# Two packed attentions: queries' and keys' parts by direct SBUF transfers, and three sets of slots

## The chip, the cores and the metric

One core of a Trainium2 chip runs the whole program in one launch. The time is the device time of an execution in microseconds (us); of several runs the median is given. PE is the engine of the matmuls, DVE, ACT and POOL work elementwise, SP only issues DMAs; ACT can issue DMAs too, on a queue of its own (ACTq; SP's is SPq).

## The reference

Eight layers run one after the other on x of 4 x 256 tokens by 128. The change concerns two of them, both attentions, which the kernel computes with one function:

```
L0: masked attention, 8 heads of 16; queries from x, keys and values from the context
    k, v = split((ctx @ W_src.T + b_src) * mask);  q = (tgt @ W_tgt.T + b_tgt) * mask
    out = softmax(q k^T / sqrt(16), masked keys at -inf) v;  [tgt, out] @ W_out.T + b_out
L1: unmasked attention, 16 heads of 8; keys and values are 256 rows of context, then 256 of x
    q, k, v from x @ w_qkv.T;  out = softmax(q k^T / sqrt(8)) v;  out @ w_proj.T + b_proj
```

Between them lies a layer of routed experts (four rounds), behind them five layers more, which the change leaves as they are. Sums are in f32.

## The kernel before

Both attentions come from packed_attention(). A query or key in f32 is split into three bf16 parts, high, middle and low (qp and kp, [128 partitions, 1024 tokens] each; a partition is one dimension of one head). The product of two such numbers is made of six terms (TERMS: pairs of part numbers), and all six are done by one matmul with a longer contraction: for a head, the six terms lie below each other on partitions. These stacks are the slots: QS and KS hold for one b (256 tokens) all heads, row r * HD + d on the partitions for term r and dimension d, heads and tokens along a row. Masked: HD = 16, 96 rows and one for the mask. Unmasked: HD = 8, 48 rows, twice (SIDES = 2: heads lie on partitions 0 and up, and on 64 and up), and KS also takes the parts of the context. Three more rows take the row maxima of the scores, in bf16 parts as well, so that the second product comes out with the maximum subtracted.

Getting the parts into the slots moves them across partitions. The kernel before goes by way of DRAM. Each term row of each half of the tokens is stored from 128 partitions (line 318): the keys by SP into k_dram, the queries by ACT into q_dram. SP waits for the stores and loads slots: masked, load_terms (line 674), seven DMAs for each b; unmasked, load_rows (line 664), in two shares of two sides for keys, queries and context each, twelve DMAs for a b. The masked attention has a set of slots for each of the four b (BUFS = 4), the unmasked one has BUFS = 2 and reloads them.

Then a software pipeline runs on all engines over the steps i (masked 16 steps, unmasked 64): first_pass (PE, line 368) makes scores of step i, DVE takes their row maxima (line 802), and once a unit of half a b is done, PE turns its maxima (425), which are split into parts (masked: ACT 539 and 571, DVE 816 and 823; unmasked: ACT 543 and POOL 623 to 628), and SP brings them to their slot rows by 2 KB transfers from SBUF to SBUF (line 733: three for a unit, six in the unmasked case). second_pass (PE, line 382) makes the scores again, LAG steps behind, after its wait for these transfers; ACT takes the exponential (555), PE multiplies by the values (412). Each engine's program is one fixed order; PE's order puts second_pass of step i - LAG behind first_pass of step i, and ahead of the next ones.

SP's order is written out by hand: for the unmasked attention the context of b = 0, the stores of the keys' first half, the loads of b = 0 (first share), the stores of the second half, all other loads of the first BUFS b, and then the loop over units v with the transfers of maxima (line 733), a piece of later weights (l1v, line 3428), and, from v = 2 on, the loads of b + 1 ahead of the unit's maxima. The buffers NMp of the maxima's parts are two, so the parts of unit v are written only after the transfers of unit v - 2.

ACT's part of the start is in scalar(): for each of the two halves it casts the first and the second part (lines 505 and 509), then issues the stores of the queries (three masked, six unmasked), and only then goes on with the next half. DVE subtracts (764 and 769). The slots are first filled with ones by POOL (those of the unmasked attention in the rounds, at line 1550, once a step).

Of the kernel before, what the change touches and what calls it, by code (L numbers as in the profile page):

```python
# [151 lines left out]
def packed_attention(k, name, number, NH, HD, key_tiles, masked, eps, W, ahead=None, split=None):  # L152
# [22 lines left out]
    BUFS = B if masked else 2  # L175
    SHARES = 1 if masked else 2
# [4 lines left out]
    SPS = SLOTS // SHARES  # L181
    HPS = NH // SHARES
# [21 lines left out]
    vtmp = k.carve(F32, HALF)  # L204
    mark = k.carve_mark()
    q32, k32 = k.carve(F32, T), k.carve(F32, T)
    qp = [k.carve(BF16, T) for _ in range(3)]
    kp = [k.carve(BF16, T) for _ in range(3)]
# [12 lines left out]
    q_dram, k_dram = k.q_dram[number], k.k_dram[number]  # L221
# [4 lines left out]

    fill_done = count("fill_done", BUFS + 1 if masked else 1)
    q_psum = count("q_psum", 2)
# [7 lines left out]
    STORES = 16 * (3 if masked else 6)  # L236
    stored_k = count("stored_k", 2 * STORES)
    stored_q = [count(f"stored_q{h}", STORES) for h in range(2)]
    c_stored = k.c_stored

    if masked:
        loaded = [[count(f"loaded{i % 2}{i // 2}", k.loads_of(name))] for i in range(BUFS)]
    else:
        loaded = [[count(f"loaded{i}{j}", 2 * k.loads_of(name)) for j in range(SHARES)] for i in range(BUFS)]
# [79 lines left out]
    def tensor(pe):  # L324
# [112 lines left out]
        for i in range(ALL + LAG + 1):  # L437
            s = i - LAG
            if i < ALL:
                b, u = divmod(i, STEPS)  # L440
                if u % (STEPS // SHARES) == 0:
                    pe.wait_ge(*loaded[b % BUFS][u // (STEPS // SHARES)].at(k.loads_of(name) * (b // BUFS + 1)))
                first_pass(b, PER * u)
# [50 lines left out]
    def scalar(act):  # L494
        k.norm.scalar(act, use, k.xnT)

        for pair in range(2):
# [12 lines left out]
            parts, cols = piece(2 * pair + 1)[2:]  # L510
# [36 lines left out]
        for i in range(ALL + LAG + 1):  # L547
# [11 lines left out]
            if s > 0 and s % key_tiles == 0:  # L559
                hg = s // key_tiles  # L560
                if hg == 1:
                    act.wait_ge(*stored_k.at(2 * STORES))
                    act.wait_ge(*stored_q[0].at(STORES))
                    act.wait_ge(*stored_q[1].at(STORES))
# [81 lines left out]
    def sync(sp):  # L646

        def store_half(h):
            for i in range(3):
                if i < 2:  # L650
                    sp.wait_ge(*part.at((first_of, last_of)[i](2 * h)))
                else:
                    sp.wait_ge(*rest.at(last_of(2 * h)))
                parts, cols = piece(2 * h)[2:]
                for row in [i] if masked else K_ROWS[i]:
                    store(sp, k_dram, NH, parts[i], row, cols).then_inc(stored_k.semaphore, 16)

        def load_rows(dram, dst, first, b, share, done):

            slots = slice(share * SPS, (share + 1) * SPS)  # L660
            for side in range(SIDES):
                h = share * HPS + side * SPS
                src = dram.rearrange("(h r) t -> r h t", h=NH)[:, h:h + SPS, b * S:(b + 1) * S]
                sp.dma_start(dst[rows_at(side, R_MASK), slots, first:first + S], src).then_inc(done, 16)

        def load_terms(dram, dst, b, parts, done):

            src = dram.rearrange("(h r) t -> r h t", h=NH)[:, :, b * S:(b + 1) * S]
            at = 0
            while at < len(parts):  # L670
                n = 1
                while at + n < len(parts) and parts[at + n] == parts[at] + n:
                    n += 1
                sp.dma_start(dst[at * HD:(at + n) * HD, :, :], src[parts[at] * HD:(parts[at] + n) * HD]).then_inc(done, 16)
                at += n

        def load_context(b, share):
            sp.wait_ge(c_stored, 16 * 6)
            load_rows(k.c_dram, KS[b % BUFS], 0, b, share, loaded[b % BUFS][share].semaphore)

        def load(b, share):
            done = loaded[b % BUFS][share].semaphore
            if b == 0:
                sp.wait_ge(*stored_k.at(STORES))
                sp.wait_ge(*stored_q[0].at(STORES))
            if b == 2:
                sp.wait_ge(*stored_k.at(2 * STORES))
                sp.wait_ge(*stored_q[1].at(STORES))
            if b >= BUFS:
                sp.wait_ge(*p2_psum.at(STEPS * (b - 2) + STEPS // SHARES * (share + 1)))  # L690
            if masked:
                load_terms(k_dram, KS[b], b, [term[1] for term in TERMS], done)
                load_terms(q_dram, QS[b], b, [term[0] for term in TERMS], done)
            else:
                load_rows(k_dram, KS[b % BUFS], NK - S, b, share, done)
                load_rows(q_dram, QS[b % BUFS], 0, b, share, done)
            if not masked and b > 0:
                load_context(b, share)

        if masked:  # L700
            sp.wait_ge(k.mask_ready, 1)
            for b in range(BUFS):
# [3 lines left out]
                    .then_inc(loaded[b][0].semaphore, 16)  # L706
        else:
            sp.wait_ge(*k.slots_filled.at(4))
            for share in range(SHARES):
                load_context(0, share)  # L710
        store_half(0)
        load(0, 0)
        store_half(1)
        for share in range(1, SHARES):
            load(0, share)
        for b in range(1, BUFS):
            for share in range(SHARES):
# [564 lines left out]
def routed_rounds(k, name, number, E, W, ahead):  # L1282
# [49 lines left out]
    k.slots_filled = k.count("packed_fill_done", 4)  # L1332
# [208 lines left out]
    def gpsimd(pool):  # L1541
        k.norm.gpsimd(pool, use)
        for g in range(ITEMS):
# [4 lines left out]
            if FILL_AT <= g < FILL_AT + 4:  # L1548
# [1618 lines left out]
class Kit:  # L3167


    def __init__(self, nc, ctx, dram):  # L3170
# [30 lines left out]
        self.q_dram = {n: dram["scratch"](f"q_parts{n}") for n in (0, 2)}  # L3201
        self.k_dram = {n: dram["scratch"](f"k_parts{n}") for n in (0, 2)}
# [112 lines left out]

    def loads_of(self, name):

        return 16 * (3 + 4 + 1 if name == "l0x" else 6)
# [140 lines left out]

def pick(width):  # L3460
# [25 lines left out]
def pack(i):  # L3486
# [4 lines left out]
    w["l0x"] = [tiles(src[:D].T), tiles(src[D:].T), f["L0_xattn_W_tgt"].T, wo[:, :D].T, tiles(slots(wo[:, D:].T, 8)),  # L3491
                pick(16), f["L0_xattn_b_src"][:D, None], f["L0_xattn_b_tgt"][:, None],
                across(f["L0_xattn_b_src"][D:]), across(f["L0_xattn_b_out"])]
    qkv = f["L1_xattn_w_qkv"]
    w["l1x"] = [qkv[D:2 * D].T, qkv[2 * D:].T, qkv[:D].T, tiles(slots(by_steps(f["L1_xattn_w_proj"].T), 16)), pick(8),
# [51 lines left out]
```

## Time and profile before

| | us |
|---|---|
| median of 3 runs (range) | 1118.69 (1116.24 to 1119.89) |
| the profiled execution, its own time | 1116.3 |
| its span, first to last instruction | 1114.5 |
| masked attention, about | 10 to 91 |
| rounds of routed experts, about | 91 to 295 |
| unmasked attention, about | 295 to 454 |
| PE busy | 979.7 (88%) |
| DVE busy | 823.2 (74%) |
| ACT busy | 636.2 (57%) |
| POOL busy | 426.2 (38%) |

The profile is of one execution. Its lines give the busy time of groups of instructions; a timeline gives for a stretch each engine's instructions in order, with the idle time in front and what ended it. The issue of a DMA by SP or ACT is a piece of time on SPq or ACTq; it isn't counted as busy time of an engine. The chain is followed back from the last instruction to what released each step.

### The profile page before, as it was taken

The page shows a single profiled execution, that of the slowest core. Times are in us where ns is not written, and L with a number is a line of the kernel's source. Part 1 is how long each engine was busy: PE and PEld are TensorE (multiplying, and loading weights), DVE is VectorE, ACT ScalarE, POOL GpSimd, SP SyncE. Part 2 cuts the span into 40 slices and gives each one's busy share as a digit, 9 for nine tenths or more (in the row PEclk, how much of TensorE's full clock was granted, in tenths as well). Part 3 has the DMA queues.
Part 4 walks back from the last instruction along what each step waited for, and adds up shares of the span by engine and source line. Part 5 has one row for each costly group of instructions (what it writes and reads, how often), then busy time and mean ns, then how long its engine had stood idle before and what let it go on. Part 6 is the DMA issues. An engine that isn't in the chain of part 4 may idle for free.

```text
span 1114.5 us, 18229 instructions
## 1 busy us (share of the span) xinstructions
PE 979.7 (88%) x5958; PEld 720.5 (65%) x5958; DVE 823.2 (74%) x1980; ACT 636.2 (57%) x1594; POOL 426.2 (38%) x664
## 2 busy tenths in 40 slices
PE   5688999999759998868999999996899999998587
PEld 4457887888513434746777777775667777777465
DVE  7855898898667881698989988768665667675663
ACT  3373666766317775366797877973144666664121
POOL 8231122111121110235766767767130565654200
PEclk9697999999859998899999999997899999999789
DMA  5530211122052310300000000303000100003000
GB/s 215 139 122 1 76 39 39 39 67 62 20 170 81 98 40 20 152 1 1 1 1 1 1 1 1 151 1 121 1 1 21 57 1 2 1 14 138 1 1 20
DMA packets 32254, 53.55 MB, mean 48 GB/s; under 512 B 4192, under 2 KB 24448, under 8 KB 31008
## 3 DMA queue, kind: packets, MB, share of 16 engines
q1 hardware_dynamic: 29616, 50.03, 13.5%
q10 hardware_dynamic: 2544, 2.36, 0.7%
q8 instruction: 48, 0.79, 0.3%
q14 instruction: 46, 0.38, 0.1%
HBM read 45.33 MB, written 6.88 MB: 47 GB/s over the span
## 4 chain that ended last, share of the span: by engine, by line
PE 64%; DVE 16%; ACT 9%; issue 6%; DMA 2%; POOL 1%; SPq 1%; DVEq 0%; ACTq 0%
PE psum L1733 8%; PE psum L1356 8%; PE psum L1366 7%; ACT region_d L1795 4%; PE psum L2524 3%; PE psum L1763 3%; PE psum L2453 3%; PE psum L412 3%; PE psum L368 2%; DVE region_d L1931 2%; ACT region_c L1812 2%; PE psum L1719 2%; PE psum L2427 2%; PE psum L2469 2%; DVE null_work L2626 2%
## 5 line engine op out<-in xcount | busy, mean ns | idle before, releaser
L1733 PE MATMUL psum<-gated_parts 128*128 128x512 f32 x768 | 191.1, 400 | 18.7 <-DVE region_d L1931 15.1
L1733 PEld LDWEIGHTS psum<-gated_parts 128*128 128x128 f32 x768 | 137.0, 188 | 69.1 <-DVE region_d L1931 36.8
L2024 POOL TENSOR_TENSOR region_d<-region_d 128x256 f32<-128x256 f32 x126 | 94.6, 751 | 93.1 <-DVE region_d L1931 91.0
L1425 ACT ACTIVATE rounds_work<-psum,region_c 128x512 f32<-128x512 f32 x128 | 84.6, 688 | 28.1 <-PE psum L1356 25.9
L802 DVE TENSOR_REDUCE work<-psum 128x1 f32<-128x512 f32 x128 | 81.8, 686 | 22.0 <-PE psum L368 20.3
L1356 PE MATMUL psum<-parts,split 128*128 128x512 f32 x384 | 95.9, 400 | 0.0
L1366 PE MATMUL psum<-parts,split 128*128 128x512 f32 x384 | 93.3, 392 | 0.0
L1547 POOL CAST parts<-rounds_work 128x1024 fp32r<-128x1024 f32 x32 | 33.4, 1043 | 151.9 <-ACT rounds_work L1425 151.9
L1795 ACT ACTIVATE region_d<-psum,gated_work 128x128 f32<-128x128 f32 x256 | 75.9, 447 | 26.8 <-issue 22.2
L1479 DVE TENSOR_TENSOR parts<-rounds_work,parts 128x1024 fp32r<-128x1024 f32 x64 | 76.3, 1220 | 16.9 <-POOL parts L1547 15.9
L1795 ACT ACTIVATE region_d<-psum,ctx 128x128 f32<-128x128 f32 x256 | 73.0, 375 | 25.2 <-PE psum L1733 15.4
L2549 ACT ACTIVATE null_work<-psum,null_work 128x257 f32<-128x257 f32 x128 | 59.6, 471 | 43.8 <-DVE null_work L2613 43.8
L1356 PEld LDWEIGHTS psum<-parts,split 128*128 128x128 f32 x384 | 73.1, 192 | 15.5
L1366 PEld LDWEIGHTS psum<-parts,split 128*128 128x128 f32 x384 | 71.5, 188 | 14.7
L1931 DVE SCALAR_TENSOR_TENSOR region_d<-psum,gated_work,region_d 128x128 f32<-128x128 f32 x256 | 71.8, 344 | 11.6 <-ACT region_d L1795 7.5
L1931 DVE SCALAR_TENSOR_TENSOR region_d<-psum,ctx,region_d 128x128 f32<-128x128 f32 x256 | 71.9, 343 | 8.8 <-ACT region_d L1795 6.2
L555 ACT ACTIVATE work<-psum 128x1024 f32<-128x1024 f32 x64 | 65.2, 1024 | 22.1 <-PE psum L382 20.1
L2613 DVE TENSOR_REDUCE null_work<-psum 128x2 f32<-128x514 f32 x64 | 44.1, 689 | 32.3 <-PE psum L2453 32.3
L2738 POOL TENSOR_TENSOR null_work<-null_work 128x512 f32<-128x512 f32 x64 | 66.5, 1039 | 0.0
L368 PE MATMUL psum<-work 48*128 48x512 bf16 x128 | 51.7, 438 | 13.8 <-DMA work<-q_parts 10.7
L133 POOL TENSOR_TENSOR rstd<-var_eps,minus_half 128x4 f32<-128x4 f32 x12 | 12.3, 1024 | 126.3 <-DVE var_eps L93 126.2
L368 PEld LDWEIGHTS psum<-work 48*128 48x128 bf16 x128 | 12.2, 96 | 52.1 <-DVE work L802 33.0
(450 smaller groups left out, 2190.6 us busy)
## 6 DMA issues: line engine op xcount, KB each, us to landing
rounds_work<-cw_rows SPq DMA_DIRECT2D x32, 256.0 KB, 3.4
region_a<-in_l1v SPq DMA_DIRECT2D x8, 512.0 KB, 4.0
region_b_last<-in_l1o SPq DMA_DIRECT2D x1, 4096.0 KB, 12.3
region_a<-in_l2f SPq DMA_DIRECT2D x1, 4096.0 KB, 12.0
region_b_last<-in_l3f_small SPq DMA_DIRECT2D x1, 4096.0 KB, 12.8
region_a<-in_l3f SPq DMA_DIRECT2D x1, 2080.0 KB, 7.4
region_c<-in_l0f SPq DMA_DIRECT2D x1, 2076.0 KB, 12.3
region_c<-in_l3x SPq DMA_DIRECT2D x1, 2048.0 KB, 7.8
```

What stands on the lines that cost most here:

```text
L368: ins = pe.matmul(bank[g % 2][:, j * NK:(j + 1) * NK], QS[b % BUFS][rows_at(side, R_MAX), slot, t * P:(t + 1) * P], KS[b % BUFS][rows_at(s ...
L555: act.activation(PT[s % 2].rearrange("p (a n) -> p a n", a=2), k.pair(2 + 2 * (s % 2)), ACT.Exp, scale=scale).then_inc(p2_exp.semaphore, 1)
L802: dve.tensor_reduce(NM[:, b, heads[0]:heads[0] + HPG, t], bank[g % 2][:, :].rearrange("p (j n) -> p j n", j=HPG), AX.X, ALU.max, negate=Tr ...
L1356: ins = pe.matmul(bank[f], w1_part[a][:, e, f * P:(f + 1) * P], cur_part[b][:, half_of(s % 2)], start=n == 0, stop=n == len(PASSES) - 1)
L1366: ins = pe.matmul(bank[4 + g % 2], w2_part[a][:, g % E, f, :], hidden_part[b][g % 2][:, f, :], start=f == 0 and n == 0, stop=f == FT - 1 a ...
L1425: act.activation(H[g % 2][:, f, :], bank[f], ACT.Gelu_apprx_tanh, bias=W("b1")[:, (g % E) * FT + f:(g % E) * FT + f + 1]).then_inc(h_ready ...
L1479: dve.tensor_tensor(two(hidden_part[1][g % 2], c), two(H[g % 2], c), two(hidden_part[0][g % 2], c).bitcast(F32), ALU.subtract).then_inc(h_ ...
L1733: ins = pe.matmul(bank[2 * (n % 2) + c], src[a][:, t * P:(t + 1) * P], weights[b][:, piece(c)], start=m == 0, stop=m == len(PASSES) - 1)
L1795: ins = act.activation(scaled[n % RING][:, e, :], bank[2 * (n % 2)][:, e * P:(e + 1) * P], ACT.Copy, scale=scalars[:, n % NT, e:e + 1])
L1931: ins = dve.scalar_tensor_tensor(out=tile, in0=bank[2 * (n % 2) + 1][:, e * P:(e + 1) * P], scalar=scalars[:, n % NT, HALF_E + e:HALF_E + ...
L2024: pool.tensor_tensor(tile[:, 0:2, :], tile[:, 0:2, :], tile[:, 2:4, :], ALU.add).then_inc(k.pool_chain, 1)
L2738: pool.tensor_tensor(PR[g % 4][:, :, 0:S], PR[g % 4][:, :, 0:S], r.broadcast_to([P, TPB, S]), ALU.mult)\
```

## The change

It sends the parts straight from qp and kp to the slots, from SBUF to SBUF. For each part, each term row that uses it, each side and each b there is one transfer (to_slots), 128 or 64 partitions of 256 tokens to HD partitions by all the heads of a side. For that the projections' columns are reordered on the host (inside_out, by_sides) so that heads run fastest inside a dimension. ACT issues the queries of b = 0, SP everything else; the stores, k_dram and q_dram go, and so do the waits for them. The unmasked attention gets three sets of slots (BUFS = 3), all loaded ahead of the loop over the units; the loads of b = 3 stand in that loop, keys and context at v = 3 and queries at v = 4. One wait for the whole of a b takes the place of one for each share. ACT casts the second half without issuing anything for it. The third set of slots is filled by two more memsets of POOL in the rounds. The buffers qp and kp no longer lie under those that the pipeline uses.

```diff
-    BUFS = B if masked else 2
-    SHARES = 1 if masked else 2
+    BUFS = B if masked else 3
+    DIRECT = 2 * len(TERMS) * SIDES
+    LOADS = 16 * (DIRECT + (1 if masked else 4))
...
+    def to_slots(queue, what, b, i):
+
+        parts, slots, first = (kp, KS, NK - S) if what == "k" else (qp, QS, 0)
+        for r in (K_ROWS if what == "k" else Q_ROWS)[i]:
+            for side in range(SIDES):
+                at = side * SIDE + r * HD
+                queue.dma_start(slots[b % BUFS][at:at + HD, :, first:first + S],
+                                parts[i][side * (P // SIDES):(side + 1) * (P // SIDES), b * S:(b + 1) * S])\
+                    .then_inc(loaded[b % BUFS].semaphore, 16)
...
-                for row in [i] if masked else Q_ROWS[i]:
-                    store(act, q_dram, NH, parts[i], row, cols).then_inc(stored_q[pair].semaphore, 16)
+                if pair == 0:
+                    if i == 0:
+                        act.wait_ge(*slots_ready)
+                    to_slots(act, "q", 0, i)
...
+        def load(b, what):
             for i in range(3):
+                parts_made(what, b // 2, i)
+                to_slots(sp, what, b, i)
...
-        store_half(0)
-        load(0, 0)
-        store_half(1)
-        for share in range(1, SHARES):
-            load(0, share)
-        for b in range(1, BUFS):
-            for share in range(SHARES):
-                load(b, share)
+            load_context(0)
+        for b in range(BUFS):
+            load(b, "k")
+            if b > 0:
+                load(b, "q")
+                if not masked:
+                    load_context(b)
         for v in range(UNITS * B):
             b, heads, _ = unit_of(v)
-            if BUFS <= b + 1 < B and b > 0:
-                load(b + 1, v % UNITS)
+            if BUFS < B and v == UNITS * (BUFS - 1) - 1:
+                sp.wait_ge(*p2_psum.at(STEPS * (B - BUFS)))
+                load(B - 1, "k")
+                load_context(B - 1)
+            if BUFS < B and v == UNITS * (BUFS - 1):
+                load(B - 1, "q")
...
-            if FILL_AT <= g < FILL_AT + 4:
+            if FILL_AT <= g < FILL_AT + 6:
```

## Rows read from the trace of the kernel before

**Rows 1.** The page, part 4: shares of the chain that ended last.

```profile
PE 64%; DVE 16%; ACT 9%; issue 6%; DMA 2%; POOL 1%; SPq 1%; DVEq 0%; ACTq 0%
```

**Rows 2.** The chain, unmasked start: start us, us, what.

```profile
308.03 2.69 DMA q_parts<-work
...
312.11 3.34 DMA work<-q_parts
```

**Rows 3.** Timeline of PE; columns: start us, us, engine line op tiles xcount [idle before <-releaser].

```profile
34.06 1.01 PE L368 MATMUL psum<-front_work 97*128 97x256 bf16 x4 [4.86 <-DMA front_work<-q_parts]
...
315.58 0.61 PE L368 MATMUL psum<-work 48*128 48x512 bf16 x2 [10.66 <-DMA work<-q_parts]
...
333.57 0.71 PE L382 MATMUL psum<-work 51*128 51x256 bf16 x3
```

**Rows 4.** Timeline of SP's queue (SPq), masked attention.

```profile
19.38 2.31 SPq L318 DMA_DIRECT2D k_parts<-front_work  x3
...
43.61 6.53 SPq L733 DMA_DIRECT2D front_work<-front_work  x9
```

**Rows 5.** Single lines: engine op xcount: issue ns min/median/max, first and last start.

```profile
L733 SPq DMA_DIRECT2D work<-work x48: 634/635/692, 328.3 to 420.5; - x48
...
L318 SPq DMA_DIRECT2D k_parts<-work x12: 528/614/960, 303.0 to 316.5; - x12
...
L664 SPq DMA_DIRECT2D work<-k_parts x16: 308/443/536, 310.8 to 384.6; - x16
...
L1558 SPq DMA_DIRECT2D cw_rows<-rounds_work x8: 264/265/284, 110.1 to 267.5; - x8
```

**Rows 6.** Timeline of SP's queue, unmasked attention.

```profile
302.95 3.82 SPq L318 DMA_DIRECT2D k_parts<-work  x6
...
322.16 0.93 SPq L664 DMA_DIRECT2D work<-k_parts  x2
...
328.34 4.13 SPq L733 DMA_DIRECT2D work<-work  x6
...
359.04 0.85 SPq L664 DMA_DIRECT2D work<-k_parts  x2
...
367.05 4.43 SPq L733 DMA_DIRECT2D work<-work  x6
...
379.51 4.05 SPq L733 DMA_DIRECT2D work<-work  x6
```

**Rows 7.** Timelines of ACT and of DVE, masked attention.

```profile
23.15 1.15 ACT L505 ACTIVATE front_work<-front_work 128x512 bf16<-128x512 f32 x2 [2.18 <-issue]
...
46.85 0.27 ACT L539 ACTIVATE front_work<-psum 8x128 bf16<-8x128 f32 x1 [1.80 <-DMA front_work<-front_work]
...
34.68 1.29 DVE L802 TENSOR_REDUCE front_work<-psum 128x2 f32<-128x512 f32 x2 [2.38 <-PE psum L368]
...
47.22 0.27 DVE L816 TENSOR_TENSOR front_work<-psum,front_work 8x128 f32<-8x128 f32 x1
```

**Rows 8.** Timelines of ACT and of DVE, unmasked start.

```profile
308.70 1.09 ACT L505 ACTIVATE work<-psum 128x512 bf16<-128x512 f32 x2 [3.47 <-issue]
...
310.71 1.29 DVE L769 TENSOR_TENSOR work<-work 128x512 bf16<-128x512 f32 x2
316.20 11.02 DVE L802 TENSOR_REDUCE work<-psum 128x1 f32<-128x512 f32 x16 [4.20 <-PE psum L368]
```

**Rows 9.** The chain, 356 to 375 us: the fourth unit's maxima reach PE.

```profile
370.84 1.68 DMA work<-work
```

**Rows 10.** The page, part 5: POOL's casts in the rounds, busy, mean, idle before.

```profile
L1547 POOL CAST parts<-rounds_work 128x1024 fp32r<-128x1024 f32 x32 | 33.4, 1043 | 151.9 <-ACT rounds_work L1425 151.9
```

**Rows 11.** DMA queue q1: packets, MB, share of 16 engines, 31:45 and 342.3:346.3.

```profile
q1 hardware_dynamic: 5892, 3.01, 92.5%
...
q1 hardware_dynamic: 64, 0.01, 1.2%
```

**Rows 12.** Stretch 316:334: us, busy (x) by engine, PEclk, DMA share, GB/s.

```profile
316.00:334.00 18.00, 15.21 (x34) 3.71 (x33) 15.57 (x24) 0.68 (x3) 1.92 (x6) 0.50 0.48 136
```

More of the change, by code:

```diff
@@ L203, in packed_attention @@
     NMf = [k.carve(F32, P) for _ in range(2)]
-    vtmp = k.carve(F32, HALF)
+    vtmp = k.carve(F32, HALF) if masked else None
+    if not masked:
+        qp, kp = ([k.carve(BF16, T) for _ in range(3)] for _ in range(2))
     mark = k.carve_mark()
     q32, k32 = k.carve(F32, T), k.carve(F32, T)
-    qp = [k.carve(BF16, T) for _ in range(3)]
-    kp = [k.carve(BF16, T) for _ in range(3)]
+    if masked:
+        qp, kp = ([k.carve(BF16, T) for _ in range(3)] for _ in range(2))
     k.carve_back(mark)
@@ L235, in packed_attention @@
     c_rest = count("c_rest", 2 if masked else 0)
-    STORES = 16 * (3 if masked else 6)
-    stored_k = count("stored_k", 2 * STORES)
-    stored_q = [count(f"stored_q{h}", STORES) for h in range(2)]
     c_stored = k.c_stored
[L241 to L244, printed above, removed]
+    loaded = [count(f"loaded{i % 2}{i // 2}", (B - i + BUFS - 1) // BUFS * LOADS) for i in range(BUFS)]
     v_sb = count("v_sb", B)
@@ L440, in tensor @@
                 b, u = divmod(i, STEPS)
-                if u % (STEPS // SHARES) == 0:
-                    pe.wait_ge(*loaded[b % BUFS][u // (STEPS // SHARES)].at(k.loads_of(name) * (b // BUFS + 1)))
+                if u == 0:
+                    pe.wait_ge(*loaded[b % BUFS].at(LOADS * (b // BUFS + 1)))
                 first_pass(b, PER * u)
@@ L560, in scalar @@
                 hg = s // key_tiles
[L561 to L564, printed above, removed]
+                if masked and hg == 1:
+                    for b in range(B):
+                        act.wait_ge(*loaded[b].at(LOADS))
                 act.wait_ge(*av_done.at(hg * key_tiles))
@@ L646, in sync @@
     def sync(sp):
-        def store_half(h):
-            for i in range(3):
[L650 to L677, printed above, removed]
-            sp.wait_ge(c_stored, 16 * 6)
-            load_rows(k.c_dram, KS[b % BUFS], 0, b, share, loaded[b % BUFS][share].semaphore)
@@ L681, in load, with parts_made @@
[L681 to L698, printed above, removed]
+        def parts_made(what, half, i):
+            m = 2 * half + (what == "q")
+            if i < 2:
+                sp.wait_ge(*part.at((first_of, last_of)[i](m)))
+            else:
+                sp.wait_ge(*rest.at(last_of(m)))
@@ new lines, in load, with load_context @@
+        def load(b, what):
+            for i in range(3):
+                parts_made(what, b // 2, i)
+                to_slots(sp, what, b, i)
+        def load_context(b):
+            sp.wait_ge(c_stored, 16 * 6)
+            for share in range(2):
+                slots = slice(share * SLOTS // 2, (share + 1) * SLOTS // 2)
+                for side in range(SIDES):
+                    h = share * NH // 2 + side * SLOTS // 2
+                    src = k.c_dram.rearrange("(h r) t -> r h t", h=NH)[:, h:h + SLOTS // 2, b * S:(b + 1) * S]
+                    sp.dma_start(KS[b % BUFS][rows_at(side, R_MASK), slots, 0:S], src).then_inc(loaded[b % BUFS].semaphore, 16)
@@ L1331, in routed_rounds @@
     high_pool = k.count("rounds_h_high", ITEMS)
[L1332 removed]
+    k.slots_filled = k.count("packed_fill_done", 6)
     FILL_AT = 8
```

26 lines of the change are left out of this document (11 added, 15 removed).

## The prediction

> **What bounds the kernel now.** I read the page's chain first: PE holds 64% of the path, DMA only 2% [rows 1]. So a change that touches only DMAs can win what the two packed attentions wait for at their starts, and little more. The chain of the unmasked attention shows it: the parts are stored (2.69 us to land), then loaded back (3.34 us) [rows 2], and PE starts its first scores at 315.58 after 10.66 us of idle; in the masked one it starts at 34.06 after 4.86 us, released by a DMA too [rows 3]. After that no load of slots is waited for again.
>
> The second view is SP's own timeline, since SP issues most of what the change replaces. SP works in order, and the 2 KB transfers of the maxima (L733) stand behind the slot loads in its program: masked, behind the loads of all four b; unmasked, behind those of the first BUFS of them. Their first issue is at 43.61 [rows 4] and at 328.34 [rows 6]. The question is what stands ahead of them after the change.
>
> **The price of one direct transfer.** The trace of before has no transfer from 128 (or 64) partitions to 16 (or 8) partitions of SBUF. Its nearest rows [rows 5]: SBUF to SBUF, L733, takes the queue 0.634 us though it moves only 2 KB; SBUF to DRAM from 128 partitions with the heads split off, L318, 0.614 us; DRAM to slots, L664, 0.443 us. The least on SP is L1558, 0.264 us. Between two issues lie 0.044 us (a pair of L664 takes 0.93 [rows 6]). I take L733's price, because both ends are SBUF as in the change: a pitch of 0.634 + 0.044 = 0.68 us. Bounds: 0.49 (L664's median) and 0.74 (L733's longest, 0.692). The context loads stay at 0.487.
>
> **Masked attention.** Removed: 6 stores on SP, 6 on ACT, 28 loads on SP. Added: 6 transfers on ACT (q of b = 0) and 42 on SP (k of b = 0, then k and q of three b, 6 each). SP is free for them at 19.38, behind its mask transfers [rows 4]. So the first transfer of maxima is issued at 19.38 + 42 x 0.68 = 47.94 instead of 43.61: 4.3 us later. Who waits: ACT's L539 for the third unit writes into a buffer that this transfer reads; it started at 46.85, released by a DMA; DVE's L816 at 47.22 needs it, and the next row maxima stand behind it in order [rows 7]. There was no slack (L816 shows no idle before it: DVE came to it straight from the row maxima), so DVE is late by 4.3 us, and PE and ACT with it.
>
> The gain at this stage's start is swallowed by that. It would be: DVE sits idle for 2.38 us before the maxima at 34.68 [rows 7], so it could start them at 32.30. ACT now has six transfers of q to issue, not three, ahead of its casts at 23.15, which move by some 1.3 us (an estimate: three more at 0.68, less the waits that lie between the present three); DVE, which needs them and has other work meanwhile, passes on some 0.8. The maxima start about 1.6 us earlier, and then stop at the third unit until the same time as above. Masked: +4.3 us; 42p - 24.2 in general for a pitch p, but never below -1.6.
>
> **Unmasked attention.** Removed: 12 stores on SP, 12 on ACT; 32 loads. Added: 12 transfers on ACT and 12 on SP for b = 0 (two sides each), and 24 each for b = 1, 2 and 3 on SP. With three sets, the loads of b = 0, 1 and 2 all stand ahead of the first transfer of maxima: 12 + 24 + 24 direct ones and 8 for the context (those of b = 0 are out long before). From SP's first store now, at 302.95 [rows 6]: 302.95 + 60 x 0.68 + 8 x 0.487 = 347.65, instead of 328.34: 19.3 us later. PE's first second_pass (L382) started at 333.57 [rows 3], 5.2 us after that issue, when the six had landed; it stands in PE's order ahead of further first passes, so DVE and ACT run dry too. It now starts at about 352.9. LAG is unchanged, so the first pass has got no further by then, and nothing is made up: +19.3 us, 60p - 21.5 in general.
>
> The gain at the start is hidden under it again, and small: ACT casts at 308.70, after waiting 3.47 us for its own six issues; six more at 0.68 make that 312.8, and DVE's last part moves from 312.0 to about 316.1, against maxima that start at 316.20 now [rows 8]. The store's and the load's landing go, ACT's longer issue is late next: -0.1 us, which the sum leaves out.
>
> Later: the loads of b = 3. SP is let go for them by the count that lets it go at 359.04 now. Then 12 x 0.68 + 4 x 0.487 = 10.1 us stand ahead of the transfers of unit 3, which go out at 367.05 [rows 6], with the chain running through them to the landing at 372.52 and on to PE [rows 9]. They go at 369.15: +2.1 us. The 12 for q come behind them: 369.15 + 4.6 + 8.2 = 381.9, against 379.51 + 2.1 = 381.6 for unit 4: +0.3. Together +2.4.
>
> POOL's two more memsets of slots fall in the rounds, where it sits idle 151.9 us in front of 32 casts, 4.7 us each [rows 10]; nothing, unless a cast came late by their length. The weight columns are reordered on the host. The third set brings b = 2 forward, but no load was waited for in the steady part: nothing.
>
> **DMA engines.** The slots take the same 512 B packets as before, and the stores go. Between 31 and 45 us 5892 packets kept 16 engines busy 92.5%, 35 ns each; the maxima's small packets from SBUF to SBUF took 12 ns (1.2% of 4 us for 64) [rows 11]. A masked transfer has 128 packets, 8 per engine, 0.28 us; that is below 0.68, so the issue bounds it.
>
> **Sum.** 4.3 + 19.3 + 2.4 = 26.0 us. Against the profiled execution (1116.3 us, span 1114.5) that is 1142.3; the median of the three runs lies 2.4 above it, inside their scatter of 3.7. I take 1118.7 + 26.0 = 1144.7, rounded to 1144.
>
> **Rivals.**
> 1. *A direct transfer is issued like a load from DRAM* (pitch 0.49). For: L664 splits heads and rows as the new destination does. Against: L733 and L318, whose two sides are cut differently, as the new ones are. Masked -1.6, unmasked 60 x 0.49 - 21.5 = +7.9, later 0: 1125.
> 2. *Not slower: the issue is cheap and the landings decide.* At L664's least, 0.308 (pitch 0.35), the masked start gains all of 2.4, the maxima's transfers go out at 302.95 + 60 x 0.35 + 3.9 = 327.9, 0.4 earlier: 1116. At L1558's 0.264 (pitch 0.31) they go at 325.5 and 2.9 us are kept: 1113. It decides below a pitch of 0.38, and is faster by over 0.3% below 0.34. Against: none of these rows splits a partition axis.
> 3. *The packets bound it.* If a packet of 512 B from SBUF to SBUF took 0.12 us, 8 per engine would take 0.96 us; 60 of them instead of 40.8 us take 57.6, 16.8 more, and masked 42 take 11.8 more: about 1173. It decides above 85 ns a packet. Against: 35 and 12 ns.
> 4. *The maxima don't wait*, because the order isn't as I read it: masked -1.6, unmasked -0.1, 1117. The diff leaves their loop behind the loads.
>
> The Trainium skill (DMA: Bandwidth & Descriptors, "Issuing engines are not separate DMA queues") calls the time a sequencer takes to start a DMA "usually small relative to the DMA itself". By that rule rival 2 would hold, at 1113 to 1116; rows 5 and 11 speak against it. The same page ("Why a DMA increments its semaphore by 16 and not by 1") lets a DMA use at most as many engines as divide the slowest dimension of both its sides, which would be 8 for the unmasked slots and would halve rival 3's room; no row here shows that number.
>
> **Chances.** Forecast, pitch 0.58 to 0.74 (+14 to +34: 1133 to 1152): 0.70. Rival 1: 0.13. Rival 2: 0.09. Rival 3: 0.06. Rival 4: 0.02. The range takes in the forecast and rival 1: 1124 to 1154, 0.83. Some 0.3% (3.4 us) can be told from no change. Faster: rival 2 below 0.34, 0.05. Same: the rest of it, rival 4 and a corner of rival 1, 0.07. Slower: 0.88.
>
> The granted clock was 0.50, the level of 1.2 GHz, from 316 to 334 after PE's idle [rows 12]. The new idle falls where the clock was low anyway; I add nothing, though it may cost 1 or 2 us more.
>
> **What would show it.** SP: an unbroken row of direct issues from 303 to about 348 (shifted by what the masked stage lost), each near 0.63 us, and L733 only behind it. PE: an idle of some 19 us before the first L382 of the unmasked attention, released by DMA or SP. ACT: the third L539 of the masked one at about 51. It is wrong if the issues take below 0.55 us, if PE starts that L382 at 330 to 335, or if the DMA share stands near full while SP waits.

## The result and the profile after

| | before | after |
|---|---|---|
| median, runs made together (range) | 1119.29 (1116.24 to 1121.01) | 1146.1 (1143.48 to 1153.77) |
| ratio, 95% interval | | 1.0257 (1.0225 to 1.0289) |
| profiled execution, its own time | 1116.3 | 1143.48 |
| span | 1114.5 | 1141.7 |
| mean granted clock | 0.936 | 0.921 |

The changed kernel is 26.8 us slower by the medians and 27.2 us by the two spans. In the changed kernel L321 is the direct transfer, L709 the maxima's transfer (it was L733), L387 the second pass (L382), L373 the first pass (L368), L673 the context's load.

The page's chain first. SP's DMA issues, 1% of it before [rows 1], now hold 6%; the page puts 4% on L321 alone:

```profile
PE 61%; DVE 14%; ACT 9%; issue 6%; SPq 6%; POOL 1%; ACTq 1%; DMA 1%; DVEq 0%; POOLq 0%
```

The next lines are single lines of the kernel (ns of one issue: least, median, most), which answer rows 5:

```profile
L321 SPq DMA_DIRECT2D work<-work x84: 608/609/936, 306.6 to 403.7; - x84
L321 SPq DMA_DIRECT2D front_work<-front_work x42: 547/598/1169, 19.3 to 46.4; - x42
L321 ACTq DMA_DIRECT2D work<-work x12: 624/705/1154, 308.6 to 316.9; - x12
```

SP's timeline, masked and then unmasked, which answers rows 4 and 6:

```profile
19.30 27.67 SPq L321 DMA_DIRECT2D front_work<-front_work  x42
...
306.61 24.70 SPq L321 DMA_DIRECT2D work<-work  x36
331.36 1.90 SPq L673 DMA_DIRECT2D work<-ctx_parts  x4
333.31 15.61 SPq L321 DMA_DIRECT2D work<-work  x24
348.96 2.13 SPq L673 DMA_DIRECT2D work<-ctx_parts  x4
351.13 4.08 SPq L709 DMA_DIRECT2D work<-work  x6
...
391.86 4.08 SPq L709 DMA_DIRECT2D work<-work  x6
...
406.35 4.08 SPq L709 DMA_DIRECT2D work<-work  x6
```

The queue never rests between 306.61 and 355.21. The first maxima go out 44.52 us behind the first issue of the stage, where before it was 328.34 - 302.95 = 25.39 [rows 6]. The maxima of unit 3 are then 24.8 us behind those of before (391.86 against 367.05), those of unit 4 26.8 (406.35 against 379.51); from there on the distance stays at 26.8.

PE's timeline at the second pass, which answers the third row of rows 3; the number in brackets is the idle time in front:

```profile
356.32 0.61 PE L387 MATMUL psum<-work 51*128 51x256 bf16 x4 [17.59 <-DMA work<-work]
...
397.05 0.39 PE L387 MATMUL psum<-work 51*128 51x256 bf16 x4 [2.09 <-DMA work<-work]
```

Both idles end with a landing of maxima, not of slots: the view of L709 names PE's L387 as waiting for it, 20.7 us in three waits, and the view of L321 names nobody. Stretches around them (us, busy by engine in the order PE, PEld, DVE, ACT, POOL, then the granted clock, DMA share, GB/s):

```profile
338.80:356.00 17.20, 0.00 (x0) 0.00 (x0) 0.66 (x1) 1.11 (x1) 0.00 (x0) 0.50 0.20 56
356.30:366.00 9.70, 9.32 (x68) 2.97 (x68) 6.13 (x10) 5.54 (x7) 1.00 (x4) 0.61 0.18 56
385.00:396.80 11.80, 9.87 (x101) 3.78 (x100) 8.83 (x14) 7.14 (x9) 1.41 (x4) 1.00 0.22 61
397.50:405.00 7.50, 7.50 (x55) 2.97 (x54) 4.47 (x7) 4.10 (x5) 0.00 (x0) 0.54 0.35 110
```

While SP issues without a pause, the DMA engines are 20% busy: it is the issuing that takes the time, not the moving. And behind the short idle of 2.09 us PE runs at 0.54 of its clock for some 7 us, which nothing in the prediction had foreseen at this place.

At the starts, ACT and DVE, masked (answers rows 7) and unmasked (rows 8):

```profile
50.26 0.27 ACT L545 ACTIVATE front_work<-psum 8x128 bf16<-8x128 f32 x1 [5.49 <-DMA front_work<-front_work]
50.56 0.28 DVE L792 TENSOR_TENSOR front_work<-psum,front_work 8x128 f32<-8x128 f32 x1 [3.54 <-ACT front_work L545]
...
308.56 9.05 ACTq L321 DMA_DIRECT2D work<-work  x12
317.65 1.09 ACT L510 ACTIVATE work<-psum 128x512 bf16<-128x512 f32 x2 [8.81 <-issue]
...
320.88 4.07 DVE L778 TENSOR_REDUCE work<-psum 128x1 f32<-128x512 f32 x6
```

### The profile page after: what moved, and what is told of

It reads as the page before. It is cut to its first block, busy times and chain, and to the rows that moved or that the text cites. A ratio compares the mean times of both kernels' runs of the same rounds, so it can differ in the third digit from the quotient of the medians.

```text
span 1141.7 us, 18274 instructions
## 1 busy us (share of the span) xinstructions
PE 986.7 (86%) x5958; PEld 725.4 (64%) x5958; DVE 823.5 (72%) x1980; ACT 637.6 (56%) x1594; POOL 430.1 (38%) x666
## 4 chain that ended last, share of the span: by engine, by line
PE 61%; DVE 14%; ACT 9%; issue 6%; SPq 6%; POOL 1%; ACTq 1%; DMA 1%; DVEq 0%; POOLq 0%
PE psum L1709 9%; PE psum L1332 7%; PE psum L1342 7%; SPq L321 4%; ACT region_d L1771 4%; PE psum L2500 3%; PE psum L2429 3%; PE psum L1739 3%; PE psum L417 2%; DVE region_d L1907 2%; ACT region_c L1788 2%; PE psum L1695 2%; PE psum L2403 2%; PE psum L2445 2%; DVE null_work L2602 2%
## 5 line engine op out<-in xcount | busy, mean ns | idle before, releaser
L1709 PE MATMUL psum<-gated_parts 128*128 128x512 f32 x768 | 193.9, 405 | 16.6 <-DVE region_d L1907 12.8
L1709 PEld LDWEIGHTS psum<-gated_parts 128*128 128x128 f32 x768 | 139.3, 191 | 67.6 <-DVE region_d L1907 34.4
L373 PE MATMUL psum<-work 48*128 48x512 bf16 x128 | 52.6, 451 | 14.8 <-ACT work L514 11.1
L387 PE MATMUL psum<-work 51*128 51x256 bf16 x256 | 36.2, 288 | 20.7 <-DMA work<-work 20.7
```

What stands on the lines that cost most here:

```text
L1709: ins = pe.matmul(bank[2 * (n % 2) + c], src[a][:, t * P:(t + 1) * P], weights[b][:, piece(c)], start=m == 0, stop=m == len(PASSES) - 1)
```

## The experiments

The theory: SP issues one after the other at 0.65 to 0.69 us, and what stands ahead of the maxima's transfers in its program decides when the second pass starts. Rivals: the transfers themselves (their number, their form, the engines' load) slow the stage wherever they stand; or the third set of slots does. Several runs each, of kernels made together with runs of the kernel before.

### One attention at a time

`e1_masked_alone`: the masked attention as changed, the unmasked one by the old function.

```diff
- stages.append(packed_attention(k, "l1x", ...))
+ stages.append(packed_by_dram(k, "l1x", ...))
```

> The masked attention sends its parts directly, the unmasked one goes by DRAM with two sets as before. Theory A (SP's queue: 42 direct issues at a pitch of 0.66 us stand ahead of the first transfer of maxima): that transfer goes out at about 47.0 us instead of 43.6, the third unit's cast starts at about 50.3 instead of 46.9, and the kernel is 3.4 us slower (1122 to 1123). Theory B (the lost microseconds of the masked attention are made up later, and the whole loss is the unmasked one's): no change, within 1 us.

Measured: 1119.36 us against 1116.45, ratio 1.0025 (1.0005 to 1.0044), so 2.8 us. SP's timeline of this kernel:

```profile
19.10 28.01 SPq L321 DMA_DIRECT2D front_work<-front_work  x42
```

The interval is 0.6 to 4.9 us: it holds the 3.4 of theory A and doesn't quite shut out theory B's "within 1 us". The maxima's transfers begin at 47.15, and the unmasked attention's first store at 306.67, 3.7 us behind that of before [rows 6]. One pair of traces doesn't settle such a distance, though. In the five traces whose masked attention is that of before (before, e2, e3, e9, e10), the first maxima go out between 43.61 and 45.44, and the unmasked attention's first issue on SP stands anywhere from 302.38 to 308.17; in the four with 42 direct issues (the changed kernel twice, e1, e5) the maxima go out between 47.01 and 47.60. The means of the two groups are 2.8 us apart, which is what e1's runs give.

`e2_unmasked_alone`: the other way round.

```diff
- stages.append(packed_attention(k, "l0x", ...))
+ stages.append(packed_by_dram(k, "l0x", ...))
```

> The unmasked attention sends its parts directly with three sets, the masked one goes by DRAM as before. Theory A: first transfer of maxima of the unmasked attention 44.5 us after SP's first direct issue, second pass 19 us later than before, then 2 us at unit 3 for SP's queue and 2 us more behind it while the clock is down: 23 us slower (1141 to 1143). Theory B: 27 us slower, all of the loss.

Measured: 1145.32 us, ratio 1.0236 (1.0184 to 1.0288), so 26.3 us with 6 to either side. The first maxima's transfer stands 352.30 - 308.17 = 44.1 us behind the first issue, as in the whole change:

```profile
308.17 24.68 SPq L321 DMA_DIRECT2D work<-work  x36
...
352.30 4.54 SPq L709 DMA_DIRECT2D work<-work  x6
```

The two parts make 0.25% + 2.36% = 2.6%, the whole 2.57%: they add up within these intervals, and some nine tenths lie in the unmasked one. The 23 us of theory A and the 27 us of theory B are both inside the interval. In its profiled execution the distance to before is 18.7 us at the first maxima and 26.0 at unit 3 (398.32 - 308.17 against 367.05 - 302.95): 2 of the 7.3 between them are unit 3's issues, the rest came in a stretch of low clock behind the main idle (granted 0.67 over 357 to 386) that was longer than in the changed kernel's execution. The interval takes in both. The same trace has a short wait at unit 3 as well, and it cost more than in the changed kernel: PE waits 3.13 us at 403.54, the granted clock is 0.50 from there to 420 and 0.82 over 420:430, and the maxima of unit 4 fall 15.73 us behind those of unit 3 (before 12.46), those of unit 5 another 16.60 behind them (before 12.65).

### The third set of slots by itself

`e3_three_sets_alone`: the kernel before, still by way of DRAM, with three sets of slots.

```diff
-    BUFS = B if masked else 2
+    BUFS = B if masked else 3
```

> Both attentions by DRAM as before, only the unmasked one has three sets, with the loads of b = 2 ahead of the loop over the units. Theory A (only the number of issues ahead of the maxima counts, at 0.487 us for a load from DRAM): 12 loads more, so SP is free at 325.0 + 5.8 = 330.9 instead of waiting until 328.3: 2.5 us slower. Theory B (the third set is where the loss is, whatever the price of an issue): 10 us or more slower. Theory C (three sets are worth something by themselves): faster.

Measured: 1122.84 us, ratio 1.005 (1.0015 to 1.0084), so 5.6 us (1.7 to 9.4): theory A's 2.5 lies inside, theory B's 10 or more does not. SP's timeline:

```profile
302.44 3.75 SPq L319 DMA_DIRECT2D k_parts<-work  x6
...
330.11 4.12 SPq L734 DMA_DIRECT2D work<-work  x6
```

The first maxima go out 27.7 us behind the first store, 2.3 more than before: 12 more loads at 0.487 are 5.8 us, and SP had waited for the maxima's parts from 325.04 to 328.34 before [rows 6], which takes 3.3 of them. So the third set costs some 2 us at this place with cheap loads; with direct transfers it puts 24 of them and four context loads ahead, 24 x 0.67 + 4 x 0.49 = 18 us. It is not the set by itself but what its filling puts in front, at this price.

### The same transfers in another order

`e4_order`: the changed kernel, every direct transfer kept, but on SP part of those of later b are moved behind the maxima of earlier units: masked, the 6 queries of b = 3; unmasked, everything of b = 2 and 3, in portions.

```diff
-        for b in range(BUFS):
-            load(b, "k")
-            if b > 0:
-                load(b, "q")
-                if not masked:
-                    load_context(b)
+        behind = {}
+        if masked:
+            for b in range(B):
+                load(b, "k")
+                if 0 < b < B - 1:
+                    load(b, "q")
+            behind = {2: [(B - 1, "q", 0)], 3: [(B - 1, "q", 1), (B - 1, "q", 2)]}
+        else:
+            load(0, "k")
+            load(1, "k"); load(1, "q"); load_context(1)
...
+            for v, n in ((1, 14), (2, 11), (3, 12), (4, 11), (5, 8)):
...
         for v in range(UNITS * B):
+            for one in behind.get(v, ()):
+                issue(*one)
```

> The changed kernel with all its direct transfers, in another order on SP: masked, the queries of b = 3 behind the maxima of the first two units; unmasked, only b = 0 and 1 ahead of the first maxima, and the transfers of b = 2 and 3 dealt out in portions of 8 to 14 between the units. Theory A (order and price on SP's queue are the whole loss): no stall before the first second pass; the masked start gains 1 us, the unmasked start loses 1 us to ACT's dearer issues: within 2 us of the kernel before (1117 to 1121). Theory B (direct transfers themselves are slow to land or crowd the DMA engines): at least 10 us slower than before still.

Measured: 1123.43 us, ratio 1.0058 (1.0027 to 1.0088). SP's timeline:

```profile
19.20 23.90 SPq L323 DMA_DIRECT2D front_work<-front_work  x36
43.14 4.14 SPq L737 DMA_DIRECT2D front_work<-front_work  x6
...
300.48 24.41 SPq L323 DMA_DIRECT2D work<-work  x36
324.94 1.90 SPq L692 DMA_DIRECT2D work<-ctx_parts  x4
326.91 4.08 SPq L737 DMA_DIRECT2D work<-work  x6
```

The masked maxima go out at 43.14 (before 43.61), the first unmasked ones 26.4 us behind the stage's first issue (before 25.4, changed 44.5). Of 2.57% only 0.58% are left. This is the run that decides between the theory and the first rival: as many transfers, of the same form, on the same queue, and nearly four fifths of the loss are gone. The time is above the 1117 to 1121 of theory A; the loss of 3 to 10 us that the interval allows stays below the 10 us and more of theory B.

`e4_again`: the same kernel, one execution more.

> The same kernel as e4_order once more, for its trace: its runs lay between 1116.6 and 1129.8 us, and the longer ones had a lower mean granted clock. Theory A (SP's order is put right and what is left is the clock's doing): whatever the time, the transfers of maxima go out at the same distances from SP's first direct issue as in the first trace, except where the granted clock is at 1.2 GHz in one trace and not in the other. Theory B (DMAs vary): the distances vary at the waits for DMAs.

Measured: 1115.36 us, first unmasked maxima at 328.88, 27.0 us behind the first issue at 301.92 (26.4 in the first trace); those of the last unit are 117.1 us behind it (116.9 in the first trace). The distances are the same in both, which is theory A. Before, the last ones were 417.11 - 302.95 = 114.2 behind: the reordered unmasked attention is still 2.7 to 2.9 us longer in this count, and the masked one in front of it isn't. This run's mean clock was 0.936, and there the kernel before takes some 1117 us. How far the clock may be set aside in such a comparison is taken up in the section on it.

### The stall at unit 3

`e5_spread_b3`: the changed kernel, only the loads of b = 3 spread over units 3, 4 and 5, in tens and eights, instead of 16 and 12.

```diff
-            if BUFS < B and v == UNITS * (BUFS - 1) - 1:
-                sp.wait_ge(*p2_psum.at(STEPS * (B - BUFS)))
-                load(B - 1, "k")
-                load_context(B - 1)
-            if BUFS < B and v == UNITS * (BUFS - 1):
-                load(B - 1, "q")
...
+            for v, n in ((3, 10), (4, 10), (5, 8)):
```

> The changed kernel, with nothing altered but the 28 loads of b = 3: 10, 10 and 8 of them ahead of the maxima of units 3, 4 and 5, instead of 16 and 12 ahead of those of units 3 and 4. Theory A (the two microseconds between unit 3 and unit 4 come from the granted clock, which falls after PE's wait of 2.1 us): without that wait the clock stays, and the last second pass comes 4 us earlier against SP's first direct issue than in the changed kernel. Theory B (only SP's lateness counts): 2 us earlier. The stall of 19 us at the first second pass stays in both: 18 to 23 us slower than before.

Measured: 1146.69 us, ratio 1.0222 (1.0132 to 1.0313), 15 to 35 us slower, too wide to show 4 us. The trace of one execution:

```profile
382.71 3.97 SPq L739 DMA_DIRECT2D work<-work  x6
...
398.53 4.08 SPq L739 DMA_DIRECT2D work<-work  x6
...
410.65 4.08 SPq L739 DMA_DIRECT2D work<-work  x6
```

From unit 3's maxima to unit 4's it takes 12.1 us (the changed kernel 14.5, before 12.46), and PE has no wait in front of unit 3's second pass: both the 2 us of the wait and the 2 us behind it are gone. The total didn't follow, and the 4 us that theory A expected at the last second pass can't be read, since in this execution the low clock lasted longer behind the main idle:

```profile
354.00:385.00 31.00, 29.48 (x190) 10.29 (x190) 16.80 (x26) 14.92 (x19) 3.31 (x10) 0.50 0.12 36
```

`e9_late_unit3`: to see the short wait without the long one, the kernel before with 12 small transfers more on SP, ahead of unit 3's maxima.

```diff
+            if not masked and v == 3:
+                more = vtmp
+                ctx = k.ctxT[:, 0, :]
+                for n in range(12):
+                    rows, cols = slice(n % 6 * 16, n % 6 * 16 + 16), slice(n // 6 * P, n // 6 * P + P)
+                    sp.dma_start(more[rows, cols], ctx[rows, cols]).then_inc(nm_loaded[3 % 2].semaphore, 16)
```

> The kernel before, with nothing of the change in it, but with 12 small transfers more on SP's queue (16 partitions of 256 bytes or so each, from ctxT to vtmp) ahead of unit 3's row maxima in the unmasked attention, so that these come late. It puts the short wait of the changed kernel into a kernel that has not had the long one. 12 issues at 0.60 to 0.61 us are 7.3 us; the slack of these maxima before is not all used, so that I expect PE to wait 1 to 5 us at the first matmul of the second pass of unit 3. Theory A (after a wait of PE of some 2 us the chip grants the low clock for a while, as the changed kernel's 0.54 in 397.5:405 shows): behind the wait there is a stretch of some 5 to 10 us with PEclk near 0.5, and unit 4's maxima come later than before by the wait and some 2 us more. Theory B (the low stretch at unit 3 of the changed kernel is a late remnant of its long wait 40 us earlier): PEclk stays at 1.00 behind the wait, and unit 4 is later by the wait alone. Time by A: 1119 to 1123 us; by B 1117 to 1121.

`e10_late_unit5`: the same two units later.

> The same 12 transfers ahead of unit 5's row maxima instead of unit 3's: the same short wait at another place of the same stage. Theory A (low clock behind any short wait of PE) expects the wait of 1 to 5 us and behind it 5 to 10 us near 0.5, with 2 us lost beside the wait; theory B (only a remnant of an earlier long wait) expects 1.00 behind the wait. If the low stretch is there at one of the two places only, it hangs on more than the length of the wait.

Measured: e9 1127.81 us with a ratio of 1.0046 (1.0012 to 1.0079), some 5 us; e10 1125.54 in one execution. PE of the first and of the second:

```profile
379.74 0.61 PE L387 MATMUL psum<-work 51*128 51x256 bf16 x4 [2.93 <-DMA work<-work]
```

```profile
403.56 0.39 PE L387 MATMUL psum<-work 51*128 51x256 bf16 x4 [3.07 <-DMA work<-work]
```

And the stretches, first e9's before and behind its wait, then e10's:

```profile
366.00:374.00 8.00, 7.91 (x80) 3.40 (x80) 6.49 (x11) 5.94 (x9) 1.40 (x4) 1.00 0.33 95
...
379.80:386.00 6.20, 6.20 (x41) 2.60 (x45) 2.69 (x5) 2.71 (x4) 0.00 (x0) 0.50 0.64 179
386.00:393.00 7.00, 6.91 (x65) 2.58 (x61) 4.81 (x8) 4.40 (x7) 1.91 (x6) 0.78 0.01 1
```

```profile
393.00:400.00 7.00, 6.91 (x71) 2.66 (x70) 6.01 (x11) 5.36 (x7) 1.40 (x4) 1.00 0.05 11
...
404.00:412.00 8.00, 7.96 (x56) 3.06 (x55) 4.46 (x7) 4.38 (x5) 0.00 (x0) 0.58 0.16 58
```

Theory A holds at both places: full clock up to the wait, 0.50 and 0.58 in the stretches behind it, full again some 7 to 9 us later. In e9 unit 3's maxima are 3.0 us late against the unit before (374.59 - 358.97 = 15.62, before 12.65), and unit 4's 3.1 more (390.15 - 374.59 = 15.56 against 12.46 before); in e10 unit 6's are 14.75 behind unit 5's where before it was 12.08, 2.7 more. A wait of 3 us costs about 6 here. (e9's median lies above both ranges: the mean clock of its profiled execution was 0.927, low elsewhere too, so the trace decides and not the time.)

`after_again`: the changed kernel once more, for a second trace.

> The changed kernel as it stands, once more, for a second trace. If the 2 us behind unit 3's wait belong to the kernel, the maxima's transfers of units 3 and 4 are again 24.8 and 26.8 us behind those of before, within 0.5 us, with a stretch at the low clock between them; if they were chance, unit 4's is again 24.8 behind, and how long the low clock lasts after the long wait at the second pass differs from the first trace.

Measured: 1145.32 us. PE waits 17.48 us at the first second pass and 2.58 us at unit 3, and the clock falls again behind it:

```profile
399.09 0.39 PE L387 MATMUL psum<-work 51*128 51x256 bf16 x4 [2.58 <-DMA work<-work]
```

```profile
400.00:404.00 4.00, 4.00 (x29) 1.84 (x23) 1.75 (x3) 1.96 (x3) 0.00 (x0) 0.50 0.47 158
```

The stage began 1.4 us later here, so the distances to before are 26.85 at unit 3 and 29.06 at unit 4, not the 24.8 and 26.8 that were expected; but their difference, 2.2 us, is what was asked: the loss behind the short wait belongs to the kernel.

### The price of an issue

`e8_probe`: the kernel before, and behind the output's transfer seven groups of eight DMAs on SP, 256 columns of bf16 each: SBUF to SBUF from 128 partitions to 16 x 8 heads, from 64 to 8 x 8, 128 to 128 unsplit, 16 x 8 to 16 x 8; DRAM to 16 x 8 in two cuts; SBUF to DRAM unsplit. Its time is of no interest.

> The kernel before, and behind its output, while all engines are idle, seven groups of eight DMAs on SP, back to back, with a wait after each group, to price an issue by form: (1) SBUF 128 partitions to 16 partitions by 8 heads, as masked; (2) 64 to 8 by 8, as unmasked; (3) 128 to 128 partitions, no split; (4) 16 to 16 partitions, 8 runs each on both sides; (5) DRAM to 16 by 8, both sides split alike; (6) the same with the DRAM side as 128 rows; (7) SBUF 128 partitions to DRAM, no split. Theory A (a split of the partition axis, where the two sides are cut differently, makes an issue dear): 1, 2 and perhaps 6 take 0.6 us, 3, 4, 5 and 7 0.33 to 0.45 us. Theory B (SBUF on both sides makes it dear): 1 to 4 take 0.6 us, the others 0.45. The kernel as a whole is 35 to 50 us longer by the added work.

Measured, single lines:

```profile
L3123 SPq DMA_DIRECT2D region_a<-xn x32: 540/599/650, 1116.0 to 1140.4; - x32
L3123 SPq DMA_DIRECT2D region_a<-ctx_parts x16: 537/598/600, 1143.5 to 1155.0; - x16
L3123 SPq DMA_DIRECT2D k_parts<-xn x8: 332/432/433, 1157.6 to 1160.9; - x8
```

Neither theory held. The first line holds the four forms from SBUF to SBUF, the second the two from DRAM: 128 rows to 128 rows without any split cost as much as the split forms, and DRAM to SBUF as much as SBUF to SBUF. Every form that writes SBUF took 0.60 us, the one that writes DRAM 0.43. But the loads of the kernel before also write SBUF, from DRAM, at a median of 0.443 [rows 5], so the side that is written isn't the rule either. What makes an issue cost 0.44 or 0.60 stays open.

### Fewer issues, larger ones

`e7_masked_halves`: the masked attention by direct transfers, with the slots laid out so that the keys of two b go in one transfer with rows of 1 KB; 30 issues on SP for 42. The unmasked attention as before the change.

```diff
+            queue.dma_start(halves[h][r * HD:(r + 1) * HD, :, :],
+                            kp[i][:, h * HALF:(h + 1) * HALF]).then_inc(loaded[2 * h].semaphore, 16)
```

> Masked attention by direct transfers with the keys of two b in one (512 tokens, 128 KB, rows of 1 KB instead of 512 B), so 30 issues on SP instead of 42; the unmasked one by DRAM with two sets as before. Theory A (the price is one of the issue): each of the larger transfers takes the queue 0.61 us as the small ones, SP is through at 39.1, the transfer of the first maxima isn't late (at 43 us or earlier), the masked attention is 1 us shorter than before: 1115 to 1118 where before is 1116 to 1118. Theory B (the price follows the bytes): about 1.2 us for each larger one, SP through at about 46, no better than 42 issues.

Measured: 1114.43 us against 1117.44, ratio 0.9978 (0.994 to 1.0015). Its SP, where L335 moves keys of two b and L328 queries of one:

```profile
24.47 3.82 SPq L328 DMA_DIRECT2D front_work<-front_work  x6
28.33 3.80 SPq L335 DMA_DIRECT2D front_work<-front_work  x6
32.18 8.68 SPq L328 DMA_DIRECT2D front_work<-front_work  x12
40.90 18.98 SPq L717 DMA_DIRECT2D front_work<-front_work  x16
```

Six transfers of twice the bytes take 3.80 us, six of the single size 3.82: the price is by the issue, not by the byte. The maxima's transfers go out at 40.90 (before 43.61 [rows 4]). DVE's timeline:

```profile
33.34 1.28 DVE L786 TENSOR_REDUCE front_work<-psum 128x2 f32<-128x512 f32 x2
...
46.08 0.27 DVE L800 TENSOR_TENSOR front_work<-psum,front_work 8x128 f32<-8x128 f32 x1
```

The row maxima begin 1.3 us earlier than before, and the third unit's part (L816 before, 47.22 [rows 7]) comes 1.1 us earlier: here the third unit keeps what the start has gained. In the changed kernel the row maxima began 0.5 us earlier than before (34.22 for 34.68), and the third unit came 3.3 us later.

`e7_again`: the same with more rounds.

> The masked attention by direct transfers with the keys of two b in one transfer (30 on SP's queue for 42), the unmasked one by way of DRAM as before, once more and with more rounds. If the price is by the issue, 30 x 0.60 = 18.0 us ahead of the first maxima for 24.2 before, 6 us less than before in the queue; what comes of it at the end is bounded by the next thing that is late, and the first look gave 0.998 of the time before. Theory C (the saving is real): ratio 0.996 to 0.998 with an interval that leaves out 1. Theory D (it was noise): ratio 0.999 to 1.001.

Measured: 1114.98 us against 1119.59, ratio 0.9963 (0.9935 to 0.9992). The interval leaves out 1, and the ratio is that of theory C. The first maxima go out at 40.60 in this trace. By its two ratios this version is 2 to 4 us faster than the kernel before, though the first interval (e7) reaches past 1; it is the only one here that is faster than both.

### Runs and the clock

Kernels that differ little can't be told apart by a handful of medians here, since each execution has its own mean granted clock: of the 57 runs of the kernel before that accompanied the experiments, 1114.75 us at 0.939, 1131.9 at 0.920. A straight line through these 57 falls by 0.83 us for each 0.001 of clock and leaves 1.8 us of scatter. Against that line, at equal clock, the means are: e1 +0.5, e3 +1.4, e4 -0.4, e7 -3.4 and -1.8, e9 +2.5, e2 and e5 +15. So of what e3 and e4 were slower by (6.4 and 7.0 us by the medians) most goes with runs of a lower clock.

That doesn't clear a kernel of it. The line takes away too much where a kernel lowers its own clock: e2 and e5 come out at +15, while the traces of the change show 26.8. And the reordered kernel's clock was lower than chance would easily make it: eight of its ten runs lie at 0.931 or below, and four of the 24 of the kernel before that were made with them. So e4 is 0.58% slower as it stands, and part of that probably comes with its own clock; by which of its waits, no run shows.

## Why the prediction was right, point by point

It gave 1144.0 (1124 to 1154) and slower at 0.88; the median was 1146.1.

- **Unmasked order on SP's queue, +19.3.** Measured +19.1 (44.52 - 25.39). It repeats: 44.1 to 44.7 in the four traces with this order (the changed kernel twice, e2, e5), 25.2 and 26.0 in e9 and e10. The pitch was 40.4 us for 60, 0.67, against 0.68 taken from the maxima's transfers. The second pass started 5.2 us behind that issue, as before. Right, and e4 shows the cause.
- **Masked, +4.3.** The maxima's transfers came 3.4 us later (47.01 for 43.61), ACT's and DVE's third unit 3.4 and 3.3. The pitch was 0.659; 42p - 24.2 gives 3.5. The mechanism was right, the term 0.9 too large. The gain at the start was 0.5 us and not 1.6, and it was swallowed as said. By the stage's end the distance was 3.7 in this pair of traces; over all traces and by e1's runs it is nearer 2.8 (see e1).
- **The unmasked start, -0.1.** This was wrong, without harm. The row maxima came 320.88 - 306.61 = 14.27 us behind SP's first issue, where it was 316.20 - 302.95 = 13.25: +1.0. ACT's issues cost 0.705, a pitch of 0.75, not SP's price; 12 of them are 9.05 us. It cost nothing, because the queue hides it.
- **Unit 3, +2.1.** Measured +2.0.
- **Unit 4, +0.3.** Measured +2.0. This is the most mis-sized term. The issue order was right (the 12 queries' issues end at 404.32 and the maxima go out 2.03 us after: SP waited for the maxima's parts, not they for SP); what came was the low clock behind PE's 2.09 us of idle. "I add nothing" for the clock held in this execution for the long idle, which fell where the clock was low anyway, and not for the short one, which fell into a stretch at the full clock; the "1 or 2 us more" named there was its size.
- **Sum.** 3.7 + 19.1 + 2.0 + 2.0 = 26.8, which is also the medians' difference; 26.0 was forecast. That the total is so close is in part luck: the errors of the masked term and of unit 4's term have opposite signs, and the start of the unmasked stage moves by several microseconds between executions. The term that makes up three quarters of the sum was right by its mechanism.
- **Rivals.** Rivals 1 and 2 needed a pitch of 0.49 and less: it was 0.67. By the Trainium skill's sentence that starting a DMA is usually small relative to the DMA itself (DMA: Bandwidth & Descriptors, "Issuing engines are not separate DMA queues") the time would have been 1113 to 1116; the trace disagrees, with SP issuing without a pause at a DMA share of 0.20. Rival 3 needed 85 ns a packet, and the engines were four fifths idle. Its sum was also off: an unmasked transfer is 32 KB by the profile's page of the changed kernel, 64 packets of 512 B, which is 4 for each of 16 engines and not 8, so that over the 60 unmasked ones 85 ns would not have been enough. Rival 4 fell with the order seen on SP.

## What to carry to other kernels

Count the issues that stand ahead of the first urgent transfer on an in-order queue, and price each by the nearest row of the trace: a removed trip through DRAM won nothing here, because 68 issues at a pitch of 0.49 to 0.67 us stood where 22 us had been enough. When a transfer's issue costs as much for twice the bytes, make fewer and larger ones, or put them behind what is waited for: e4 gives back nearly four fifths of the loss by order alone, and e7, with fewer and larger transfers, is 2 to 4 us faster than the kernel before. A wait of PE of 2 to 3 us in a stretch at full clock cost about twice its length in four executions here, and over three times in a fifth.

## What the runs showed of the hardware that was not expected

- Behind a wait of PE of 2.1 to 3.1 us, the granted clock fell from 1.00 to 0.50 (from the level of 2.4 GHz to that of 1.2), in five executions of four kernels. In four of them it was back 7 to 9 us later, at a cost of 2.0 to 3.1 us beside the wait; in the fifth (e2) only after more than 16 us, at a cost of 7.2 us (3.3 by unit 4, 3.9 more by unit 5).
- Behind the long idle of 17 us it stayed low for anything between some 8 us and more than 30, in executions of nearly the same program (0.61 over 356.3:366 in the changed kernel, 0.50 over 354:385 in e5).
- An issue on SP took 0.60 us for six forms of 32 or 64 KB alike, and for 128 KB as well (e7's keys, six in 3.80 us); 0.43 us from SBUF to DRAM. The same transfer issued by ACT took 0.705 (SP 0.609).
